# Attention groups of an early-fusion block: scores and value products of two steps issued together, text loads moved ahead in the DMA queue

## Reference

```python
h = h + attn(layernorm(h))   # attn(x) = x + softmax(mask(q k / 8)) v Wo, 16 heads of 64
h = h + ffn(layernorm(h))    # router, top 2 of 8 experts, capacity 570, gelu, 256 -> 1024 -> 256
```

## Time and profile before

| what | value |
|---|---|
| median of 3 runs | 967.36 us (965.38 to 967.66) |
| profiled execution, its own time | 964.54 us |
| its span, first to last instruction | 962.6 us |
| mean granted TensorE clock | 0.958 of full speed |
| busy, share of the span | TensorE 90%, VectorE 58%, ScalarE 54%, GpSimd 38% |
| start of pair 0's scores, groups 0 to 7 | 50.8, 143.7, 224.3, 304.8, 385.4, 465.9, 546.5, 622.4 us |
| length of a group, groups 1 to 5 | 80.5 us each |
| length of group 0 | 92.9 us |

### The profile page before, as it was taken

One profiled execution on the slowest core, in us unless ns is written; L12 is line 12 of the kernel. 1 busy time (PEld: TensorE's weight loads), 2 busy tenths in 40 slices (PEclk: granted clock), 3 DMA queues, 4 the chain that ended last, 5 costly groups with the idle time before them and its releaser, 6 DMA issues.

```text
span 962.6 us, 19817 instructions
## 1 busy us (share of the span) xinstructions
PE 869.2 (90%) x6897; PEld 753.9 (78%) x6897; DVE 555.8 (58%) x2433; ACT 516.0 (54%) x1686; POOL 370.4 (38%) x677
## 2 busy tenths in 40 slices
PE   4895899999999999999999999998617999999996
PEld 3674697788778779778877877876617999999996
DVE  3563428645753853764575375476326777777771
ACT  3373808825952880782495288087005555555551
POOL 2132305426425534542642554454430333222333
PEclk9797999999999999999999999999757999999998
DMA  8442101102011111110200110100125654444422
GB/s 253 118 131 78 39 1 35 38 13 64 11 29 44 33 38 39 37 39 8 59 1 1 33 35 2 37 1 2 24 90 165 165 124 127 96 131 109 94 26 25
DMA packets 61907, 57.64 MB, mean 60 GB/s; under 512 B 26783, under 2 KB 56651, under 8 KB 61696
## 3 DMA queue, kind: packets, MB, share of 16 engines
q1 hardware_dynamic: 41170, 45.15, 15.3%
q0 software_dynamic: 18944, 9.76, 6.3%
q10 hardware_dynamic: 1696, 1.49, 0.6%
HBM read 34.25 MB, written 21.89 MB: 58 GB/s over the span
## 4 chain that ended last, share of the span: by engine, by line
PE 76%; SPq 5%; DVE 5%; POOL 4%; ACT 4%; issue 3%; DMA 2%; ACTq 1%; POOLq 0%; DVEq 0%
PE bank L380 13%; PE bank L382 12%; PE bank L381 12%; PE pT_bank L1238 6%; PE o_bank L1249 6%; PE score_bank L1229 6%; PE score_bank L1127 3%; SPq L436 3%; POOL pr L570 2%; PE o_bank L380 2%; PE o_bank L381 2%; PE o_bank L382 2%; PE score_bank L380 2%; PE score_bank L381 2%; PE score_bank L382 2%
## 5 line engine op out<-in xcount | busy, mean ns | idle before, releaser
L570 POOL TENSOR_SCALAR pr<-pr,rc 114x114 f32<-114x114 f32 x512 | 179.3, 370 | 244.9 <-DVE rc L988 244.9
L703 ACT ACTIVATE pr<-sm,nb 114x114 f32<-114x114 f32 x512 | 192.2, 379 | 34.9 <-DVE nb L984 33.5
L980 DVE CUSTOM_DVE_ANT_0 sm<-score_bank,mask 114x114 f32<-114x114 f32 x512 | 110.5, 272 | 52.9 <-PE score_bank L1229 52.8
L601 POOL DMA_INDIRECT out_dram<-yout,dest x40 | 74.0, 1851 | 164.0 <-ACT yout L755 162.5
L551 POOL DMA_INDIRECT slots_dram<-rows,slot x64 | 72.8, 1138 | 128.0 <-DVE slot L947 93.3
L621 ACT ACTIVATE kT<-bank 128x456 f32<-128x456 f32 x64 | 34.1, 533 | 146.8 <-PE bank L382 146.8
L1229 PEld LDWEIGHTS score_bank<-kT,qT 64*114 64x114 f32 x1024 | 61.8, 176 | 56.7 <-issue 34.7
L380 PE MATMUL bank<-xT_hi,wqkv_hi 128*128 128x456 f32 x256 | 104.0, 406 | 0.0
L1229 PE MATMUL score_bank<-kT,qT 64*114 64x114 f32 x1024 | 84.5, 283 | 20.6 <-DVE mx L980 17.5
L703 ACT ACTIVATION_READ_ACCUMULATOR pr<-sm,nb 114x1 f32 x512 | 97.1, 190 | 0.0
L381 PE MATMUL bank<-xT_lo,wqkv_hi 128*128 128x456 f32 x256 | 94.5, 369 | 0.0
(11 more groups left out here) (198 smaller groups left out, 2227.0 us busy)
## 6 DMA issues: line engine op xcount, KB each, us to landing
stage_a<-in_L_ffn_w_dram SPq DMA_DIRECT2D x8, 1024.0 KB, 5.1
stage_b<-in_L_ffn_w_dram SPq DMA_DIRECT2D x8, 1024.0 KB, 7.2
slots_dram<-fill SPq DMA_DIRECT2D x8, 605.6 KB
xs<-slots_dram SPq DMA_DIRECT2D x8, 605.6 KB
pix<-in_x_dram SPq DMA_DIRECT2D x96, 36.0 KB, 2.2
hraw<-in_txt_dram SPq DMA_DIRECT2D x8, 308.0 KB
out_dram<-h SPq DMA_DIRECT2D x8, 308.0 KB
pix<-pix SPq DMA_DIRECT2D x7, 216.0 KB, 2.5
```

The lines of the kernel that those rows point to most:

```text
L570: p = pool.tensor_scalar(pr[:, m % 4, i, :], pr[:, m % 4, i, :], rc[:, m % 4, i:i + 1], 1.0, ALU.mult, ALU.mult)
L601: pool.indirect_dma_start(out, bass.IndirectOffsetOnAxis(ap=dest[e % 2][:, t:t + 1], axis=0), yout[:, t, :], None, compute_op=ALU.add).the ...
L703: a = act.activation(pr[:, n % 4, i, :], sm[:, n % 2, i, :], ACT.Exp, bias=nb[:, n % 2, i:i + 1], scale=SCALE, accum_out=rs[:, n % 4, i:i ...
L980: m = dve.tensor_tensor_reduce(sm[:, n % 2, i, :], score_bank[i % 2][0:T, i // 2 * T:(i // 2 + 1) * T], mask[:, :], 1.0, NEG, ALU.add, ALU ...
```

## The change

TensorE issues the scores of pairs n and n + 1 in even steps, each pair in its own half of the columns, and the values of pairs n - 4 and n - 3 in even steps too. ScalarE and VectorE take the high and low parts of these two pairs in even steps. VectorE's first maximum waits for both pairs' scores. V's second halves are all emptied at step 18, behind the last low parts. The SyncE queue issues the text of group g + 1 ahead of the pixels of g + 2, and clears the slots inside group 0's turn, behind both.

```diff
-        V_SECOND = {PAIRS + 1: (0, 1), PAIRS + 2: (2, 3)}
+        V_SECOND, V_DRAINED = {PAIRS + 1: (0, 1), PAIRS + 2: (2, 3)}, {PAIRS + 2: (0, 1, 2, 3)}
...
             load_pixels(1)
-            sp.wait_ge(fill_done, 2)
-            for e in range(E):
-                sp.dma_start(slots[...], fill[:, :, :]).then_inc(slots_cleared, 16)
-            sp.dma_start(out[...], fill[:, :, 0:D]).then_inc(slots_cleared, 16)
+            def clear_slots():
+                sp.wait_ge(fill_done, 2)
+                for e in range(E):
+                    sp.dma_start(slots[...], fill[:, :, :]).then_inc(slots_cleared, 16)
+                sp.dma_start(out[...], fill[:, :, 0:D]).then_inc(slots_cleared, 16)

             def body(g, first=False, last=False):
                 jobs = Jobs(g)
+                if not last:
+                    sp.wait_ge(hx_done, 2 * g + 2)
+                    load_text(g + 1)
                 if g < G - 2:
                     sp.wait_ge(packed, g + 2)
                     load_pixels(g + 2)
-                if not last:
-                    sp.wait_ge(hx_done, 2 * g + 2)
-                    load_text(g + 1)
+                if first:
+                    clear_slots()
...
# ScalarE
-                    if 3 <= n:
-                        m = n - 3
-                        ...
+                    if n % 2 == 0:
+                        for m in (n - 4, n - 3):
+                            if 0 <= m:
+                                c, b = m // 2, 2 * (m % 2)
+                                act.wait_ge(o_done, pair(g, m + 1))
+                                act.activation(oT_hi[...], o_bank[m % 2][:, 0:2 * T], ACT.Copy).then_inc(o_hi, 1)
...
# VectorE (the low parts in the same way as ScalarE's high parts)
-                        dve.wait_ge(scores_done, 2 * pair(g, n + 1))
+                        dve.wait_ge(scores_done, 2 * pair(g, n + 2 - n % 2))
...
-                        for b in V_SECOND.get(n, ()):
+                        for b in V_DRAINED.get(n, ()):
                             drain_v(jobs, b)
...
# TensorE
-                if n == 0 and g < G - 1:
-                    pe.wait_ge(embT_done, g + 2)
-                else:
-                    pe.wait_ge(max_done, pair(g, n))
+                    if n == 0 and g < G - 1:
+                        pe.wait_ge(embT_done, g + 2)
+                    else:
+                        pe.wait_ge(max_done, pair(g, n))
...
-                        m = pe.matmul(score_bank[h][0:T, b * T:(b + 1) * T], qT[head, c % 2, tokens], ...)
+                        m = pe.matmul(score_bank[h][0:T, tokens], qT[head, c % 2, tokens], ...)
...
-                    if n < PAIRS:
-                        scores(g, n, jobs, first)
-                    if 3 <= n:
-                        weigh_values(g, n - 3, first)
+                    if n % 2 == 0:
+                        for m in (n, n + 1):
+                            if m < PAIRS:
+                                scores(g, m, jobs, first)
+                        for m in (n - 4, n - 3):
+                            if 0 <= m:
+                                weigh_values(g, m, first)
                     if 2 <= n < PAIRS + 2:
                         transpose_probs(g, n - 2, first)
```

More of the change, by code:

```diff
@@ L433, in _ @@
             load_pixels(1)
-            sp.wait_ge(fill_done, 2)
-            for e in range(E):
-                sp.dma_start(slots[e * CAP:(e + 1) * CAP, :].rearrange("(t p) r -> p t r", p=T), fill[:, :, :]).then_inc(slots_cleared, 16)
-            sp.dma_start(out[B * T:B * T + CAP, :].rearrange("(t p) r -> p t r", p=T), fill[:, :, 0:D]).then_inc(slots_cleared, 16)
+            def clear_slots():
+                sp.wait_ge(fill_done, 2)
+                for e in range(E):
+                    sp.dma_start(slots[e * CAP:(e + 1) * CAP, :].rearrange("(t p) r -> p t r", p=T), fill[:, :, :]).then_inc(slots_cleared, 16)
+                sp.dma_start(out[B * T:B * T + CAP, :].rearrange("(t p) r -> p t r", p=T), fill[:, :, 0:D]).then_inc(slots_cleared, 16)
             def body(g, first=False, last=False):
                 jobs = Jobs(g)
+                if not last:
+                    sp.wait_ge(hx_done, 2 * g + 2)
+                    load_text(g + 1)
                 if g < G - 2:
@@ L681, in body @@
                             drain_v(jobs, b)
-                    if 3 <= n:
-                        m = n - 3
[L685 to L693, removed]
+                    if first and n == 4:
+                        act.wait_ge(filled, len(START_JOBS))
+                        act.wait_ge(wk_lo, 1)
+                        act.wait_ge(wo_lo_done, 1)
+                        act.wait_ge(cls_in, 16)
+                    if n % 2 == 0:
[3 more added lines that the diff above has]
+                                act.wait_ge(o_done, pair(g, m + 1))
+                                act.activation(oT_hi[:, c, b * T:(b + 2) * T], o_bank[m % 2][:, 0:2 * T], ACT.Copy).then_inc(o_hi, 1)
                     if 2 <= n < PAIRS + 2:
@@ L976, in body @@
                     if n < PAIRS:
-                        dve.wait_ge(scores_done, 2 * pair(g, n + 1))
+                        dve.wait_ge(scores_done, 2 * pair(g, n + 2 - n % 2))
                         for i in range(4):
-                            m = dve.tensor_tensor_reduce(sm[:, n % 2, i, :], score_bank[i % 2][0:T, i // 2 * T:(i // 2 + 1) * T], mask[:, :],
+                            m = dve.tensor_tensor_reduce(sm[:, n % 2, i, :], score_bank[i % 2][0:T, (2 * (n % 2) + i // 2) * T:(2 * (n % 2) + i // 2 + 1) * T], mask[:, :],
                                                          1.0, NEG, ALU.add, ALU.max, mx[:, n % 2, i:i + 1])
@@ L988, in body @@
                         dve.reciprocal(rc[:, (n - 1) % 4, :], rs[:, (n - 1) % 4, :]).then_inc(recip_done, 1)
-                    if 3 <= n:
[L991 to L994, removed]
+                    if n % 2 == 0:
+                        for m in (n - 4, n - 3):
+                            if 0 <= m:
+                                c, b = m // 2, 2 * (m % 2)
+                                dve.wait_ge(o_hi, pair(g, m + 1))
+                                split_low(oT_lo[:, c, b * T:(b + 2) * T], o_bank[m % 2][:, 0:2 * T], oT_hi[:, c, b * T:(b + 2) * T], o_lo)
                     if not first:
@@ L1228, in scores @@
                         head = slice(h * DK, (h + 1) * DK)
-                        m = pe.matmul(score_bank[h][0:T, b * T:(b + 1) * T], qT[head, c % 2, tokens], kT[head, c % 2, tokens], start=True, stop=True)
+                        m = pe.matmul(score_bank[h][0:T, tokens], qT[head, c % 2, tokens], kT[head, c % 2, tokens], start=True, stop=True)
                         if b == 1:
```

## The result

The changed kernel takes 974.64 us (median of 4 runs, 972.44 to 975.80), the kernel before 967.25: ratio 1.0078, 95% interval 1.0054 to 1.0101. The change makes the kernel slower by 7.4 us, where 8.8 us of gain were forecast. The span goes from 962.6 to 970.5 us.

A forecast was written before the change was run, and what follows sets the result against it. TensorE sets the pace, ScalarE not far behind. Group 0 -12.9, groups 1 to 5 +5.0, group 6 0, group 7 -0.9: total -8.8 us, 955.7 profiled, median 958.5 us, range 949.5 to 963.5.

The forecast's parts named there:

- Part 1: Group 0, text issued ahead: 11.45 us of TensorE idling and 1.98 us of low clock go, together 13.4 us.
- Part 2: TensorE's saving per two steps from fewer tiling mode switches: 0.19 + 0.16 + 0.09 = 0.44 us of 5.81.
- The 0.09 in front of a block of scores: Last projection product takes 0.30 us ahead of scores, 0.21 ahead of a full-array transposition: 0.09 us saved.
- the 0.26 us: Estimated duration of one matmul, used to work out a 114-column pass: (0.94 - 0.26) / 7 = 0.10 us.
- Part 3: What the new order makes late: work behind an even step's scores and values starts 0.4 or 0.8 us later.
- an ordinary turn: TensorE waits 0.22 us ahead of the odd step's transposition, so the turn gains 0.22 us instead of 0.44.
- steps 10 and 11: Transposition, `pack` and K come later: +0.79 us in groups 0 to 5; groups 6 and 7 gain 0.22.
- steps 12 and 13: X starts later and step 14's scores wait for a maximum behind X's split: +0.70 us; group 0: 0.
- ahead of V's last product: Step 18: V's last product waits about 1.0 us for a drain; balance of steps 14 to 18 +0.16 us.
- the turn with `AT_Y`: Steps 8 and 9: extra TensorE work in step 8 covers the wait, so the full 0.44 us is gained.
- group 7: +0.2 - 0.44 - 0.44 - 0.22, last steps without V neither gaining nor losing: -0.9 us.
- rival D: Idle gaps in steps 11 and 13 drop the clock to 1.2 GHz, groups 0 to 5: 24 us, 982 us; 4%.

The follow-up runs named there:

- work in the idle time: Changed kernel plus 8 unread matmuls on the identity at the end of step 13, groups 1 to 6: 960.04 us, ratio to before 0.9925.
- three small moves on VectorE and ScalarE: Changed kernel with step 13's maximum ahead of logits and X's split, packing in step 17, step 18's routing ahead of the low parts: 929.73 us, ratio 0.9619.
- the kernel with hx later: Kernel with the three small moves, GpSimd's second addition of hx moved from step 1 to behind pair 1's scaling: 927.96 us, ratio to before 0.9601.

## Why the prediction was wrong

**Part 1 was right.** 13.4 us forecast; 12.8 measured alone (13.5 in the turn of steps 8 and 9 itself), and 13.8 on group 0 within the changed kernel, where 12.9 was forecast for that group as a whole. What was moved behind the text cost nothing, as costed.

**Part 2 was right as far as the rows show it.** Of the saving of 0.44 us a turn, 0.34 is in the starts of the blocks: two pairs' scores and values together take 1.92 us, where twice the single blocks would be 2.26. The 0.09 in front of a block of scores shows in no row by itself. No row gives the 0.26 us that the pass was worked out with; the pass itself comes out of the doubled block, (0.99 - 0.58) / 4 = 0.10 us.

**Part 3 had the waits and their sizes.** Turns in us, forecast against measured in group 4: an ordinary turn 5.59 (5.81 less 0.22) against 5.62 and 5.68; steps 10 and 11, 7.19 against 7.18; steps 12 and 13, 8.52 against 8.52. The wait ahead of odd transpositions, for K, for the maximum and ahead of V's last product were forecast at 0.2, 1.5, 2 and 1.0 and measured at 0.2 to 0.3, 1.4, 2.0 and 0.8. Without the clock's part (work in the idle time) groups 1 to 5 take 81.9 to 82.1, where 80.5 + 1.0 = 81.5 was forecast. Two terms were off: the turn with `AT_Y` gained 0.1, not 0.44, since the projection's bank in step 9 is emptied by a ScalarE that is late (the 0.68 us between 410.07 and 410.75 above, where 0.37 is usual), and group 7 lost 0.7 in steps 12 and 13 like the others, where I had given it no loss.

**The step that failed is the judgement on rival D, and with it the sum's price for the clock, which was nothing.** The prediction had the gap ahead of step 14's scores right (2 us) and charged only the wait. The runs showed a fall of the clock there in each of groups 1 to 6, worth 12.0 of the 16.7 us between forecast and measurement. Rival D had named the place, and I gave it 4% because the clock had not fallen behind one gap of 2.10 us. That row was one case, and it doesn't repeat: with the text order alone the same gap was followed by the low level (last section), and the gap of 2.7 us in group 0 of the paired kernels was followed by full clock in the changed kernel and by the low level in the run with work in the idle time. So from such a row a chance can't be set near nothing.

Rival D wasn't right in its working either. It counted two gaps; the low level came only with the second. Its price was 4 us a group in groups 0 to 5, against 1.5 to 2.8 us measured in groups 1 to 6.

That the idle time of step 13 brings the fall in groups 1 to 6 is shown by filling it. Why it came in all six, in the changed kernel and in the one with the paired order alone, and in group 0 only at times, is open. One difference is that TensorE does the router logits ahead of the gap in groups 1 to 6, 1.5 us of products of 8 columns, and none in group 0. No run tests that, and the fall in group 0 of the run with filler shows that it also comes without them.

The account against the forecast, in the profiled spans: forecast -8.8, measured +7.9, a difference of 16.7. The clock in groups 1 to 6 is 12.0 of it, the rest of groups 1 to 5 about 1.9, group 6 0.5, group 7 and what follows 2.3, the start of the kernel 0.9, and group 0 gives 0.9 back.

The Trainium skill, TensorE: Matmul & The Clock Gate, Part 1, says that TensorE throttled is the default and activity is what releases it. The traces agree: with 8 products that nobody reads in the gap, the clock stayed at 1.00 in groups 1 to 6. The prediction had named the warning that this part gives about idle gaps, and weighed it below a single row.

## What to carry to other kernels

When a reordering makes TensorE faster, work out the new gaps, and price each of them with a fall of the clock and without: here a gap of 2 us cost its own length and then 1.5 to 2.8 us more. When results come earlier on one engine, the lists of the others have to be reordered too; here the pairing cost 20 us with the old lists, and with three small moves on VectorE and ScalarE the paired kernel takes 929.7 us, against 950.0 for the unpaired one with its text ahead and its packing late. How much of these 20 us the two moves on VectorE's list would have brought without pairing is open. And one row that shows no fall of the clock is one case and no bound.

## What was not expected of the hardware

The same gap does not always bring the fall. In the kernel before, the step behind 106.86 ran at full clock after 2.10 us of idling (scores 0.66 us); in the kernel with the text order alone the same step, after 2.11 us, ran at the low level:

```profile
95.38 1.12 PE L1232 MATMUL score_bank<-kT,qT 64*114 64x114 f32 x8 [2.11 <-DVE mx L983]
96.42 1.03 PE L1252 MATMUL o_bank<-pT,vv 114*64 114x114 f32 x8
```

Group 0 of the paired kernels shows the same with a gap of 2.7 us (94.58 and 95.64, above): full clock in the changed kernel, the low level in the run with work in the idle time.

And VectorE's scaling of 4 maxima, usually 0.17 us, takes up to 1.30 us while GpSimd's addition of hx runs (367.38, 1.28 us, above), here in the kernel with hx later:

```profile
365.69 0.17 DVE L973 TENSOR_SCALAR nb<-mx 114x4 f32<-114x4 f32 x1
...
367.38 1.30 DVE L973 TENSOR_SCALAR nb<-mx 114x4 f32<-114x4 f32 x1
```

It takes 0.78 us in the kernel before (391.29, beside `hx` at 390.77) and 0.46 in the changed one (389.64), and each time it ends 0.02 to 0.03 us behind the addition, while VectorE's maxima beside the same addition keep their 0.27 us. So moving a GpSimd instruction out of its own chain can put it in front of VectorE's. The Trainium skill, Advanced Engine Details and Errata, Mode Summary, says that VectorE's second SBUF port is shared with GpSimd, and that GpSimd's instructions and those of VectorE that use both ports block each other. These rows agree in time; no run here shows whether the scaling uses both ports, or separates the port from other causes.
